# A selective-scan stage on one core: an output norm's shift and a copy moved to ScalarE, exponentials put ahead, and a residual taken apart on GpSimd

## The chip, the cores and the metric

The kernel runs on one core of a Trainium2 chip. The metric is the device time of one execution in microseconds (us); lower is better. Engines are named as in the profile: PE is TensorE, DVE is VectorE, ACT is ScalarE, POOL is GpSimd, SP is SyncE.

## The reference

Two layers on x of 16 x 256 x 128 (float32). Layer 0 is a retention recurrence and a mixture of experts, layer 1 a selective scan (Mamba) and a top-2 mixture of experts. The change touches the scan alone:

```python
# per sequence of 256 rows; h is the modulated layer norm of x
proj = h @ W_in.T                      # x_s (256), z (256), B (16), C (16), dt (8)
x_s  = silu(conv4(x_s) + conv_b)
dt   = softplus(dt @ W_dt.T + b_dt)
A    = -exp(A_log)
# for t in 256 steps, for each of 256 channels d and 16 states n:
#   S[d,n] = exp(dt[d] * A[d,n]) * S[d,n] + dt[d] * B[n] * x_s[d]
#   y[d]   = sum_n S[d,n] * C[n]
y    = (y + x_s * D) * silu(z)
out  = h + y @ W_out.T
out  = (out - mean) * rsqrt(var + 1e-5) * ln_g + ln_b
x    = x + ga * out
```

## The kernel before

`scan_phase` works through B = 16 sequences, one after the other. A sequence has 8 steps, j = 0 to 7 (SCAN_J), of two states each. In each engine's program `body(b, k, first, prepares)` is one sequence: it runs the 8 steps of sequence b, finishes sequence b-1 (its output product, norm and residual, `finish`) and prepares sequence b+1 (`prepare`). Every engine keeps its own fixed order, and semaphores join them. Sequence 0 finishes nothing, sequence 15 prepares nothing, and `last` finishes sequence 15.

One step j of sequence b: POOL writes dt*u*B, transposed, for two states into `dbuT` (`inputs`, four instructions, three steps ahead of use). PE turns it into a PSUM bank (`turn_inputs`). ACT writes exp(dt*A) into `dA` (`decays`, four instructions, three steps ahead, in a ring of four). DVE runs the recurrence over time (`recur`, one scan of 1024 elements, L1229) and multiplies by C (`times_C`, L1240). PE spreads C over the partitions (`C_rows`, L1614) and sums the states in PSUM (`sum_states`, L1644). In steps 0, 1 and 3 POOL takes half of the product with C (`shared_C`, L1498), and DVE's scan two steps later waits for it.

Preparing b+1: ACT normalises x (`xn`, L1279), PE transposes it, ACT modulates it to `hT` (L1285), PE projects it (L1550), ACT copies out the rows `low`, `BT` and `bc` (`prepare(1)`), and POOL splits `bc` into bfloat16 parts (`split`, L1419 to L1424, in its step 6). `C_rows(b+1, 0)` on PE waits for that split. PE projects the step sizes (L1560), ACT makes abs, positive part, exponential, square and logarithm of them (`prepare(2)`), POOL the cubic (`cubic`, L1435 and L1440), DVE the smaller of the two (`lesser`, L1200), POOL `dt` (L1446). PE runs the convolution (L1568), ACT loads the table of silu and makes `u` and `z` from it, loads its first table again (`prepare(4)`), makes `decays(7)` and then copies `dtuT` (L1319, `prepare(5)`), which PE has transposed (L1584) from POOL's `dtu` (L1460). POOL's `inputs(b+1, ..., 0)` starts in its step 5 and waits for `dtuT`. `hres` is a copy of `hT` for the residual product (`keep`, L1454).

Finishing b-1: DVE multiplies by z (`yz`, L1206), PE transposes it and multiplies by W_out (L1594 to L1604), DVE takes mean and variance of the output (`omv`, step 2), ACT the reciprocal deviation (`orstd`, L1329 and L1331), DVE the shift -mean*orstd (`oshift`, L1220), ACT the normalised output (`oh`, L1336), and POOL adds it to x with three instructions (`residual`, L1466, L1469, L1474) in its step 5, ahead of `inputs(b+1, ..., 0)`.

Of the kernel before, what the change touches and what calls it, by code (L numbers as in the profile page):

```python
# [20 lines left out]
P = 128  # L21
# [71 lines left out]
def pause(eng, passed):  # L93

    eng.sem_inc(passed, 1)
# [30 lines left out]
def setup_phase(nc, d, m, ps):  # L126

    with ExitStack() as ctx:
# [71 lines left out]
        def _(dve):  # L200
# [4 lines left out]
            tick(dve.memset(m.eps[:, 3:4], -SMALL_E))  # L205
            tick(dve.memset(m.eps[:, 4:5], SQ_B))
            tick(dve.memset(m.gates[:, 0, 2 * D:3 * D], 0.0))
            tick(dve.memset(m.ones128[:], 1.0 / D))
# [896 lines left out]
def scan_phase(nc, d, m, ps):  # L1105
# [8 lines left out]
    with ExitStack() as ctx:  # L1114
        sem = semaphores(nc, ctx, "s_")

        def sb(n, s, dt=F32):
# [4 lines left out]
        ostats, omv = sb("ostats", [P, NCH, 6]), sb("omv", [P, NCH, 2])  # L1122
        olnv, orstd, oshift = (sb(n, [P, NCH]) for n in ("olnv", "orstd", "oshift"))
        xn = sb("xn", [P, NCH, D])
# [25 lines left out]
                 "cub small least e_ready sq over st rs shift xn xT h hres xs_ps bc_ps z_ps low BT "  # L1150
                 "u_ready z_ready dt_ps pos abs ln soft dt_ready dtu_ready dtuT_ps dtuT hi r1 mid bc_parts oln gate "
                 "yz yzT_ps yzT out_ps ostats ost ors oshift o_read og done "
# [17 lines left out]
        def _(dve):  # L1170
# [31 lines left out]
            def finish(step, b, k):  # L1202
                if step == 0:
                    dve.wait_ge(S["y_part"], 8 * b + 8)
                    dve.wait_ge(S["z_ready"], b + 1)
                    dve.tensor_tensor(yz[:], bY[:, :].rearrange("p (c d) -> p c d", c=NCH), z[:, k], ALU.mult)\  # L1206
                        .then_inc(S["yz"], 1)
                if step == 2:
                    dve.wait_ge(S["out_ps"], b + 1)
                    pause(dve, S["v_passed"])  # L1210
                    for c in range(NCH):
                        dve.bn_stats(ostats[:, c, :], bZ[:, c * D:(c + 1) * D]).then_inc(S["ostats"], 1)
                    dve.wait_ge(S["ostats"], 2 * b + 2)
                    pause(dve, S["v_passed"])
                    for c in range(NCH):
                        dve.bn_aggr(omv[:, c, :], ostats[:, c, :]).then_inc(S["ost"], 1)
                if step == 3:
                    dve.wait_ge(S["ors"], b + 1)
                    dve.wait_ge(S["ost"], 2 * b + 2)
                    dve.scalar_tensor_tensor(oshift[:], omv[:, :, 0], -1.0, orstd[:], ALU.mult, ALU.mult)\  # L1220
                        .then_inc(S["oshift"], 1)

# [21 lines left out]
            def body(b, k, first, prepares):  # L1244
                for j in range(SCAN_J):
                    recur(b, j)
                    if not first and j != 3:
                        finish(j, b - 1, 1 - k)
                    if prepares and j == 4:
                        lesser(b + 1)  # L1250
                    times_C(b, j, first)
                    if not first and j == 3:
                        finish(j, b - 1, 1 - k)

# [9 lines left out]
        def _(act):  # L1264
# [8 lines left out]
            def prepare(step, b, k):  # L1273
# [43 lines left out]
                if step == 5:  # L1317
                    act.wait_ge(S["dtuT_ps"], b + 1)
                    act.activation(dtuT[:, k], bX[:, :].rearrange("p (c d) -> p c d", c=NCH), ACT.Copy)\  # L1319
                       .then_inc(S["dtuT"], 1)  # L1320

            def finish(step, b, k):
# [4 lines left out]
                if step == 2:  # L1327
                    act.wait_ge(S["ost"], 2 * b + 2)
                    act.activation(olnv[:], omv[:, :, 1], ACT.Ln, bias=m.eps[:, 0:1]).then_inc(S["oln"], 1)  # L1329
                    act.wait_ge(S["oln"], b + 1)  # L1330
                    act.activation(orstd[:], olnv[:], ACT.Exp, scale=-0.5).then_inc(S["ors"], 1)  # L1331
                if step == 3:
                    act.wait_ge(S["oshift"], b + 1)
                    act.wait_ge(S["og"], 2 * b + 2)
# [16 lines left out]
            def body(b, k, first, prepares):  # L1351
                for j in range(SCAN_J):
                    if prepares and j in (4, 5):
                        prepare(j, b + 1, 1 - k)
# [4 lines left out]
                    if prepares and j == 0:  # L1359
                        prepare(0, b + 1, 1 - k)  # L1360
                        prepare(0.5, b + 1, 1 - k)
                    if prepares and j == 1:
                        prepare(1, b + 1, 1 - k)
                        prepare(2, b + 1, 1 - k)
                    if not first:
# [7 lines left out]
            act.wait_ge(S["shift"], 1)  # L1373
            for j in (0, 0.5, 1, 2, 3, 4, 5):
                prepare(j, 0, 0)
                if j == 2:
                    rstds(1, NCH, TILES)
# [33 lines left out]
        def _(pool):  # L1411
# [35 lines left out]

            def keep(b, k):

                pool.wait_ge(S["h"], b + 1)  # L1450
                if not (isinstance(b, int) and b <= 1):
                    pool.wait_ge(S["out_ps"], b - 1)
                pause(pool, S["p_passed"])
                pool.tensor_copy(hres[:, k, :], hT[:, k, BACK:]).then_inc(S["hres"], 1)  # L1454

            def times_u(b, k):
# [4 lines left out]

            def residual(b):

                pool.wait_ge(S["o_read"], 2 * b + 2)
                pool.wait_ge(S["done"], b + 1)
                pool.tensor_tensor(og[:], oh[:], gate[:, 0, bass.ds(b, 1), :].broadcast_to([P, NCH, D]), ALU.mult)\  # L1466
                    .then_inc(S["og"], 1)
                pool.wait_ge(S["og"], 2 * b + 3)
                pool.tensor_tensor(og[:], og[:], gate[:, 1, bass.ds(b, 1), :].broadcast_to([P, NCH, D]), ALU.add)\  # L1469
                    .then_inc(S["og"], 1)  # L1470
                pool.wait_ge(S["og"], 2 * b + 4)
                pause(pool, S["p_passed"])
                xs = m.x_res[:, bass.ds(b * NCH, NCH), :]
                pool.tensor_tensor(xs, xs, og[:], ALU.add).then_inc(S["done"], 1)  # L1474

            def inputs(b, k, j, free):

# [5 lines left out]
                pause(pool, S["p_passed"])  # L1483
                for c in range(NCH):
                    for n in range(2):
                        ins = pool.tensor_scalar(dbuT[:, j % RING, c, n, :], dtuT[:, k, c, :],  # L1486
                                                 BT[:, k, c, 2 * j + n:2 * j + n + 1], 1.0, ALU.mult, ALU.mult)
                ins.then_inc(S["dbuT"], 1)
# [13 lines left out]
            def body(b, k, first, prepares):  # L1502
                for j in range(SCAN_J):
# [4 lines left out]
                    if not first and j == 5:  # L1508
                        residual(b - 1)
                    if j + AHEAD < SCAN_J:  # L1510
                        inputs(b, k, j + AHEAD, not (first and j + AHEAD < RING))
                    elif prepares:
                        inputs(b + 1, 1 - k, j + AHEAD - SCAN_J, True)
                    if prepares and j == 3:
# [3 lines left out]
                    if prepares and j == 6:  # L1518
                        split(b + 1, 1 - k)
                    if prepares and j == 7:  # L1520
                        keep(b + 1, 1 - k)

# [5 lines left out]
            split(0, 0)  # L1528
            keep(0, 0)
            cubic(0)  # L1530
            steps(0, 0)
            times_u(0, 0)
            for j in range(AHEAD):
                inputs(0, 0, j, False)
            sequences(pool, body, lambda b, k: residual(b))

# [999 lines left out]
```

## Time and profile before

| | before |
|---|---|
| device time, median of 3 runs | 1308.1 us (1304.93 to 1313.24) |
| profiled execution | 1306.6 us, of it a span of 1304.8 us from first to last instruction |
| busy share of the span | PE 79%, PEld 63%, DVE 63%, ACT 52%, POOL 47% |
| DVE's scans (L1229) | 128 in 291.6 us, from 401.4 us to 865.5 us |
| POOL's `dbuT` (L1486) | 512 in 242.3 us |
| mean granted clock of PE | 0.891 |

The span holds several stages in turn; the scan stage runs from about 380 to 880 us. Within it a sequence is a period that repeats, so most of the reading is of one period, from 606 to 636 us, and of the two ends of the stage. Busy shares of the whole span say little about it.

### The profile page before, as it was taken

Reading aid. Unit: us, or ns where it says so; the run is one execution under the profiler, and the core shown is the slowest. Engines: PE = TensorE matmul, PEld = TensorE weight load, DVE = VectorE, ACT = ScalarE, POOL = GpSimd, SP = SyncE. Lnnn points to the kernel's source line nnn. Section 1 sums busy time; section 2 is a strip of 40 time slices with the busy share of each in tenths; the row PEclk is TensorE's granted clock in tenths of the full one; section 3 lists DMA queues with packets and bytes.
Section 4 is the critical chain, followed back from the end, with each engine's and each line's share of the span. In section 5 each row is a group of like instructions: output and inputs, shape, how many; then the busy total and the mean of one; then the engine's idle time right before and its main releaser. Section 6 shows DMA issues by size and latency. Waiting matters only on the chain. (4 is left out here: it accounts for less than half of the span.)

```text
span 1304.8 us, 24618 instructions
## 1 busy us (share of the span) xinstructions
PE 1030.7 (79%) x7128; PEld 820.0 (63%) x7129; DVE 828.4 (63%) x1598; ACT 676.9 (52%) x1513; POOL 615.4 (47%) x922
## 2 busy tenths in 40 slices
PE   3999829999977888888898888851743999999950
PEld 2676623667867777888888778841732666666630
DVE  3787647222356999999999999961766333333327
ACT  2566313343127888888888888712642333333310
POOL 0000004000108899999999999930110455555630
PEclk9998759899978999999999999975555999999985
DMA  6000000766120000000000000005110111111135
GB/s 204 2 2 0 1 7 32 162 160 162 33 71 20 14 13 12 12 17 19 12 12 12 12 12 12 13 0 202 32 33 7 33 38 38 38 38 37 38 83 166
DMA packets 51613, 59.08 MB, mean 45 GB/s; under 512 B 5417, under 2 KB 45298, under 8 KB 50306
## 3 DMA queue, kind: packets, MB, share of 16 engines
q1 hardware_dynamic: 41570, 41.18, 11.9%
q0 software_dynamic: 4608, 9.45, 2.6%
q10 hardware_dynamic: 5392, 7.92, 1.8%
q8 instruction: 22, 0.36, 0.1%
q14 instruction: 21, 0.17, 0.0%
HBM read 49.32 MB, written 9.21 MB: 45 GB/s over the span
## 5 line engine op out<-in xcount | busy, mean ns | idle before, releaser
L1229 DVE TENSOR_TENSOR_SCAN s_hs<-s_dA,bank 128x1024 f32<-128x1024 f32 x128 | 291.6, 2278 | 9.8 <-PE bank L1626 9.1
L1486 POOL TENSOR_SCALAR s_dbuT<-s_dtuT,s_BT 128x256 f32<-128x256 f32 x512 | 242.3, 503 | 11.3 <-POOL s_bc L1424 5.4
L1347 ACT ACTIVATE s_dA<-s_dt,aneg 128x255 f32<-128x255 f32 x512 | 211.8, 495 | 0.3
L2255 PE MATMUL bank<-w,x_xT 128*128 x288 | 128.1, 568 | 18.0 <-ACT x_xT L2297 15.6
L1626 PE MATMUL bank<-const,s_dbuT 128*128 128x128 f32 x1024 | 136.0, 277 | 3.1 <-POOL s_dbuT L1486 3.1
L1240 DVE TENSOR_TENSOR s_hc<-s_hs,bank 128x1024 f32<-128x1024 f32 (+1 forms) x128 | 130.3, 1018 | 4.8 <-PE bank L1614 1.1
L1644 PE MATMUL bank<-const,s_hc 128*128 128x128 f32 x832 | 113.6, 275 | 21.1 <-DVE s_hc L1240 21.1
L2214 POOL DMA_INDIRECT x_xg<-hf_rows,x_src x72 | 69.7, 969 | 127.7 <-issue 63.9
L2293 ACT ACTIVATE x_a<-bank 128x448 f32<-128x448 f32 x72 | 39.2, 545 | 159.3 <-PE bank L2255 156.9
L1626 PEld LDWEIGHTS bank<-const,s_dbuT 128*128 128x128 f32 x1024 | 117.0, 143 | 6.3 <-POOL s_dbuT L1486 3.6
L1644 PEld LDWEIGHTS bank<-const,s_hc 128*128 128x128 f32 x832 | 95.0, 142 | 24.9 <-DVE s_hc L1240 24.9
L2221 POOL DMA_INDIRECT y_rows<-x_y,x_dst x72 | 71.1, 987 | 29.3 <-issue 22.4
L2255 PEld LDWEIGHTS bank<-w,x_xT 128*128 128x128 f32 x288 | 50.0, 193 | 55.1 <-issue 54.5
L2277 PE MATMUL bank<-w2d,x_hT 112*128 x576 | 77.6, 277 | 2.2 <-DVE x_y L2325 2.0
L2313 DVE COPY x_src<-from_row 128x1 uint32 (+1 forms) x72 | 11.1, 154 | 98.8 <-PE bank L2264 95.4
L2277 PEld LDWEIGHTS bank<-w2d,x_hT 112*128 112x128 f32 x576 | 69.9, 191 | 4.8 <-issue 4.2
L1031 DVE COPY yT<-bank 128x512 f32 x16 | 11.1, 692 | 91.7 <-PE bank L1011 91.7
L1023 ACT ACTIVATE g<-bank 128x512 f32<-128x512 f32 x64 | 38.2, 597 | 56.7 <-PE bank L1002 56.7
L1614 PE MATMUL bank<-s_bc,spread 128*128 128x256 bf16 x208 | 44.6, 277 | 27.1 <-DVE s_hc L1240 26.7
L1568 PE MATMUL bank<-s_hT,wc 128*128 128x256 f32 x256 | 62.4, 388 | 1.3 <-ACT s_pos L1300 1.3
L1498 POOL TENSOR_TENSOR s_hc<-s_hs,s_Crow 128x512 f32<-128x512 f32 x48 | 61.8, 1286 | 0.1
L1002 PE MATMUL bank<-xin,w 128*128 x128 | 59.4, 619 | 2.8 <-POOLq L973 2.8
(300 smaller groups left out, 2103.8 us busy)
## 6 DMA issues: line engine op xcount, KB each, us to landing
xn<-prob_d SPq DMA_DIRECT2D x16, 512.0 KB, 7.8
s_Crow<-C_rows SPq DMA_DIRECT2D x48, 128.0 KB, 2.9
w<-in_w SPq DMA_DIRECT2D x16, 256.0 KB, 3.1
o_yr<-y_rows SPq DMA_DIRECT2D x8, 512.0 KB, 3.9
w<-in_w ACTq DMA_DIRECT2D x1, 3584.0 KB, 13.1
x_res<-in_x SPq DMA_DIRECT2D x4, 512.0 KB, 9.4
gate<-gates_d SPq DMA_DIRECT2D x2, 1024.0 KB, 5.8
spread<-place_d SPq DMA_DIRECT2D x8, 256.0 KB, 6.4
```

The source lines that it names most:

```text
L1229: dve.tensor_tensor_scan(flat(hs[:, j % 2]), flat(dA[:, j % RING]), bDbu[j % 2], 0.0, ALU.mult, ALU.add).then_inc(S["scanned"], 1)
L1240: dve.tensor_tensor(hc[:, j % 2, :, 0:own], hs[:, j % 2, :, 0:own], bC[:, 0:own * L].rearrange("p (n t) -> p n t", n=own).unsqueeze(1).bro ...
L1347: ins = act.activation(dA[:, j % RING, h, n, 1:], dt[:, k, h, 1:], ACT.Exp, scale=m.aneg[:, h, 2 * j + n:2 * j + n + 1])
L1486: ins = pool.tensor_scalar(dbuT[:, j % RING, c, n, :], dtuT[:, k, c, :], BT[:, k, c, 2 * j + n:2 * j + n + 1], 1.0, ALU.mult, ALU.mult)
L1498: pool.tensor_tensor(hc[:, j % 2, :, 1], hs[:, j % 2, :, 1], Crow[:, k, i, :].unsqueeze(1).broadcast_to([P, NH, L]), ALU.mult)\
L1568: mm = pe.matmul(bX[:, h * L:(h + 1) * L], m.wc[:, tap, h * P:(h + 1) * P], hT[:, k, tap:tap + L], start=(tap == 0), stop=(tap == KCONV - 1))
L1626: mm = pe.transpose(out[:, h, n, c * P:(c + 1) * P], dbuT[:, j % RING, c, n, h * P:(h + 1) * P], ident)
L1644: mm = pe.matmul(part(c, h), hc[:, j % 2, h, n, c * P:(c + 1) * P], ident, is_transpose=True, start=(j == 0 and n == 0 and c == 0 and h == 0),
L2214: pool.indirect_dma_start(xg[k][:], None, m.hf_rows[:, :], bass.IndirectOffsetOnAxis(ap=src[k][:, 0:1], axis=0)).then_inc(S["rows"][k], 16)
L2221: pool.indirect_dma_start(m.y_rows[:, :], bass.IndirectOffsetOnAxis(ap=dst[k][:, 0:1], axis=0), y[k][:], None).then_inc(S["sent"][k], 16)
L2255: mm = pe.matmul(ps[2 * k + i][:, 0:I1], xT[:, k, :], m.w13[:, bass.ds(e * 2 + i, 1), :].rearrange("p e i -> p (e i)"), start=True, stop=True)
L2277: mm = pe.matmul(ps[5][:, 0:D], hT[:, k, i, :], m.w2d[:, bass.ds(e * NIC + i, 1), :].rearrange("p e d -> p (e d)"), start=(i == 0), stop=( ...
```

## The change

Four parts, all in `scan_phase`. (1) ACT computes `oshift` itself, with three small instructions behind `orstd` (a negated `orstd`, then one product for each half), and DVE's L1220 goes; with it goes the exception that put DVE's `finish(3)` behind `times_C`. (2) The copy `hres` goes from POOL (step 7) to ACT (`prepare(6)`, at the head of its step 6). (3) ACT's `prepare(2)` moves from step 1 to step 2, behind `decays(5)`. (4) POOL's `residual` becomes three functions: the first product (`residual_gated`) stays in front of `inputs(b+1, ..., 0)`, the other two instructions go between that block's four: ts, shifted, ts, added, ts, ts. A constant is also set once (`m.eps[:, 5:6]`) that nothing reads.

```diff
@@ DVE finish
-                if step == 3:
-                    dve.wait_ge(S["ors"], b + 1)
-                    dve.wait_ge(S["ost"], 2 * b + 2)
-                    dve.scalar_tensor_tensor(oshift[:], omv[:, :, 0], -1.0, orstd[:], ALU.mult, ALU.mult)\
-                        .then_inc(S["oshift"], 1)
@@ ACT prepare
+                if step == 6:
+                    act.wait_ge(S["h"], b + 1)
+                    if not (isinstance(b, int) and b <= 1):
+                        act.wait_ge(S["out_ps"], b - 1)
+                    act.activation(hres[:, k, :], hT[:, k, BACK:], ACT.Copy).then_inc(S["hres"], 1)
@@ ACT finish, step 2
                     act.activation(orstd[:], olnv[:], ACT.Exp, scale=-0.5).then_inc(S["ors"], 1)
+                    act.wait_ge(S["ors"], b + 1)
+                    act.activation(onegative[:], orstd[:], ACT.Copy, scale=-1.0).then_inc(S["onegative"], 1)
+                    act.wait_ge(S["onegative"], b + 1)
+                    for c in range(NCH):
+                        act.activation(oshift[:, c:c + 1], omv[:, c, 0:1], ACT.Copy, scale=onegative[:, c:c + 1])\
+                           .then_inc(S["oshift"], 1)
                 if step == 3:
-                    act.wait_ge(S["oshift"], b + 1)
+                    act.wait_ge(S["oshift"], 2 * b + 2)
@@ ACT body
-                    if prepares and j in (4, 5):
+                    if prepares and j in (4, 5, 6):
                         prepare(j, b + 1, 1 - k)
...
-                    if prepares and j == 1:
-                        prepare(1, b + 1, 1 - k)
-                        prepare(2, b + 1, 1 - k)
+                    if prepares and j in (1, 2):
+                        prepare(j, b + 1, 1 - k)
@@ POOL inputs
-            def inputs(b, k, j, free):
+            def inputs(b, k, j, free, rest=None):
...
-                for c in range(NCH):
-                    for n in range(2):
-                        ins = pool.tensor_scalar(dbuT[:, j % RING, c, n, :], dtuT[:, k, c, :],
-                                                 BT[:, k, c, 2 * j + n:2 * j + n + 1], 1.0, ALU.mult, ALU.mult)
+                for i in range(2 * NCH):
+                    c, n = divmod(i, 2)
+                    ins = pool.tensor_scalar(dbuT[:, j % RING, c, n, :], dtuT[:, k, c, :],
+                                             BT[:, k, c, 2 * j + n:2 * j + n + 1], 1.0, ALU.mult, ALU.mult)
+                    if rest is not None and i == 0:
+                        residual_shifted(rest)
+                    if rest is not None and i == 1:
+                        residual_added(rest)
@@ POOL body
                     if not first and j == 5:
-                        residual(b - 1)
+                        residual_gated(b - 1)
+                    if not first and j == 5 and not prepares:
+                        residual_shifted(b - 1)
+                        residual_added(b - 1)
...
-                        inputs(b + 1, 1 - k, j + AHEAD - SCAN_J, True)
+                        inputs(b + 1, 1 - k, j + AHEAD - SCAN_J, True, b - 1 if j == 5 and not first else None)
...
-                    if prepares and j == 7:
-                        keep(b + 1, 1 - k)
```

## Rows read from the trace of the kernel before

**Rows 1.** One period: us; busy PE, PEld, DVE, ACT, POOL; granted clock, DMA, GB/s.

```profile
520.00:549.00 29.00, 25.71 (x203) 23.29 (x202) 28.17 (x24) 24.65 (x56) 27.32 (x47) 1.00 0.07 14
```

**Rows 2.** Timeline of DVE, one period: start, us, engine, line, operation, [idle before].

```profile
606.07 2.28 DVE L1229 TENSOR_TENSOR_SCAN s_hs<-s_dA,bank 128x1024 f32<-128x1024 f32 x1
...
620.07 0.90 DVE L1220 SCALAR_TENSOR_TENSOR s_oshift<-s_omv,s_orstd 128x2 f32<-128x2 f32 x1 [0.49 <-ACT s_orstd L1331]
620.90 2.27 DVE L1229 TENSOR_TENSOR_SCAN s_hs<-s_dA,bank 128x1024 f32<-128x1024 f32 x1
...
635.17 2.28 DVE L1229 TENSOR_TENSOR_SCAN s_hs<-s_dA,bank 128x1024 f32<-128x1024 f32 x1
```

**Rows 3.** Timeline of POOL in the same period.

```profile
608.73 0.41 POOL L1454 COPY s_hres<-s_hT 128x256 f32<-128x256 f32 x1
...
625.97 1.28 POOL L1460 TENSOR_TENSOR s_dtu<-s_dt,s_u 128x512 f32<-128x512 f32 x1 [0.16 <-POOL s_dt L1446]
627.20 0.73 POOL L1466 TENSOR_TENSOR s_og<-s_oh,s_gate 128x256 f32<-128x256 f32 x1
628.12 0.73 POOL L1469 TENSOR_TENSOR s_og<-s_og,s_gate 128x256 f32<-128x256 f32 x1 [0.18 <-POOL s_og L1466]
629.12 0.73 POOL L1474 TENSOR_TENSOR x_res<-x_res,s_og 128x256 f32 x1 [0.27 <-POOL s_og L1469]
629.83 3.67 POOL L1486 TENSOR_SCALAR s_dbuT<-s_dtuT,s_BT 128x256 f32<-128x256 f32 x8
...
635.00 0.67 POOL L1424 TENSOR_TENSOR s_bc<-s_r,s_bc 32x256 bf16<-32x256 f32 x1
```

**Rows 4.** Timelines of DVE and POOL around other executions of L1220.

```profile
445.15 1.27 POOL L1440 TENSOR_TENSOR s_small<-s_cub,s_e 128x512 f32<-128x512 f32 x1
...
445.21 1.23 DVE L1220 SCALAR_TENSOR_TENSOR s_oshift<-s_omv,s_orstd 128x2 f32<-128x2 f32 x1 [0.32 <-ACT s_orstd L1331]
...
852.14 0.79 DVE L1220 SCALAR_TENSOR_TENSOR s_oshift<-s_omv,s_orstd 128x2 f32<-128x2 f32 x1
...
875.93 0.16 DVE L1220 SCALAR_TENSOR_TENSOR s_oshift<-s_omv,s_orstd 128x2 f32<-128x2 f32 x1 [0.60 <-ACT s_orstd L1331]
```

**Rows 5.** Timeline of ACT in the same period.

```profile
624.54 0.84 ACT L1311 ACTIVATE s_u<-bank,bcol 128x256 f32<-128x256 f32 x2 [0.92 <-PE bank L1568]
...
628.92 0.57 ACT L1319 ACTIVATE s_dtuT<-bank 128x512 f32<-128x512 f32 x1
629.40 6.47 ACT L1347 ACTIVATE s_dA<-s_dt,aneg 128x255 f32<-128x255 f32 x16
```

**Rows 6.** Timelines of POOL, PE, ACT: end of sequence 0, sequence 1.

```profile
426.18 3.66 POOL L1486 TENSOR_SCALAR s_dbuT<-s_dtuT,s_BT 128x256 f32<-128x256 f32 x8 [2.93 <-ACT s_dtuT L1319]
...
431.43 0.67 POOL L1424 TENSOR_TENSOR s_bc<-s_r,s_bc 32x256 bf16<-32x256 f32 x1
...
425.37 0.58 ACT L1319 ACTIVATE s_dtuT<-bank 128x512 f32<-128x512 f32 x1
...
454.07 0.57 ACT L1319 ACTIVATE s_dtuT<-bank 128x512 f32<-128x512 f32 x1
...
432.23 0.28 PE L1614 MATMUL bank<-s_bc,spread 128*128 128x256 bf16 x1 [0.36 <-POOL s_bc L1424]
...
447.75 1.89 PE L1568 MATMUL bank<-s_hT,wc 128*128 128x256 f32 x8
```

**Rows 7.** Timelines of DVE, POOL, PE: both ends of the stage.

```profile
437.68 2.29 DVE L1229 TENSOR_TENSOR_SCAN s_hs<-s_dA,bank 128x1024 f32<-128x1024 f32 x1 [0.66 <-POOL s_hc L1498]
...
845.03 2.28 DVE L1229 TENSOR_TENSOR_SCAN s_hs<-s_dA,bank 128x1024 f32<-128x1024 f32 x1
...
833.40 3.66 POOL L1486 TENSOR_SCALAR s_dbuT<-s_dtuT,s_BT 128x256 f32<-128x256 f32 x8
...
404.43 0.44 PE L1545 MATMUL bank<-const,s_xn 128*128 128x128 f32 x2 [1.66 <-ACT s_xn L1279]
```

**Rows 8.** Groups of instructions, 433 to 836 us: busy, mean ns, idle before.

```profile
L1331 ACT ACTIVATE s_orstd<-s_olnv 128x2 f32<-128x2 f32 x14 | 2.9, 204 | 0.4
```

More of the change, by code:

```diff
@@ L206, in _ @@
             tick(dve.memset(m.eps[:, 4:5], SQ_B))
+            tick(dve.memset(m.eps[:, 5:6], SQ_C))
             tick(dve.memset(m.gates[:, 0, 2 * D:3 * D], 0.0))
@@ L1122, in scan_phase @@
         ostats, omv = sb("ostats", [P, NCH, 6]), sb("omv", [P, NCH, 2])
-        olnv, orstd, oshift = (sb(n, [P, NCH]) for n in ("olnv", "orstd", "oshift"))
+        olnv, orstd, onegative, oshift = (sb(n, [P, NCH]) for n in ("olnv", "orstd", "onegative", "oshift"))
         xn = sb("xn", [P, NCH, D])
@@ L1150, in scan_phase @@
                  "cub small least e_ready sq over st rs shift xn xT h hres xs_ps bc_ps z_ps low BT "
-                 "u_ready z_ready dt_ps pos abs ln soft dt_ready dtu_ready dtuT_ps dtuT hi r1 mid bc_parts oln gate "
+                 "u_ready z_ready dt_ps pos abs ln soft dt_ready dtu_ready dtuT_ps dtuT hi r1 mid bc_parts oln onegative gate "
                  "yz yzT_ps yzT out_ps ostats ost ors oshift o_read og done "
@@ L1246, in body @@
                     recur(b, j)
-                    if not first and j != 3:
+                    if not first:
                         finish(j, b - 1, 1 - k)
@@ L1251, in body @@
                     times_C(b, j, first)
-                    if not first and j == 3:
-                        finish(j, b - 1, 1 - k)
             def last(b, k):
@@ L1373, in _ @@
             act.wait_ge(S["shift"], 1)
-            for j in (0, 0.5, 1, 2, 3, 4, 5):
+            for j in (0, 0.5, 1, 2, 3, 4, 5, 6):
                 prepare(j, 0, 0)
@@ L1446, in steps @@
                 pool.tensor_tensor(dt[:, k], least[:], pos[:], ALU.add).then_inc(S["dt_ready"], 1)
[L1448 to L1454, printed above, removed]
             def times_u(b, k):
@@ L1460, in times_u, with residual_gated @@
                 pool.tensor_tensor(dtu[:], dt[:, k], u[:, k], ALU.mult).then_inc(S["dtu_ready"], 1)
-            def residual(b):
+            def residual_gated(b):
                 pool.wait_ge(S["o_read"], 2 * b + 2)
@@ L1467, in residual, with residual_shifted @@
                     .then_inc(S["og"], 1)
+            def residual_shifted(b):
                 pool.wait_ge(S["og"], 2 * b + 3)
@@ L1470, in residual, with residual_added @@
                     .then_inc(S["og"], 1)
+            def residual_added(b):
                 pool.wait_ge(S["og"], 2 * b + 4)
-                pause(pool, S["p_passed"])
                 xs = m.x_res[:, bass.ds(b * NCH, NCH), :]
                 pool.tensor_tensor(xs, xs, og[:], ALU.add).then_inc(S["done"], 1)
-            def inputs(b, k, j, free):
+            def inputs(b, k, j, free, rest=None):
                 if j == 0:
@@ L1528, in _ @@
             split(0, 0)
-            keep(0, 0)
             cubic(0)
@@ L1534, in _, with last @@
                 inputs(0, 0, j, False)
-            sequences(pool, body, lambda b, k: residual(b))
+            def last(b, k):
+                residual_gated(b)
+                residual_shifted(b)
+                residual_added(b)
+            sequences(pool, body, last)
         @block.tensor
```

## Prediction

> **What bounds the kernel now.** I read the busy time by engine in one period first, then the timelines of DVE and POOL, then what ends the short idle times. In 29.00 us DVE is busy 28.17 and POOL 27.32, PE 25.71, ACT 24.65 [rows 1]: two engines are full, so busy shares alone don't say which one sets the pace. The period is the distance of two first scans, 635.17 - 606.07 = 29.10 us [rows 2].
>
> POOL's timeline [rows 3] has no idle time that another engine ends. Its gaps (0.16, 0.18, 0.27) are waits for its own instruction before. POOL's period is thus a sum of its own work. DVE has one soft place: before L1220 it waits 0.49 us for ACT, and L1220 then takes 0.90 us on 2 columns [rows 2]. The same instruction took 0.16 us when POOL was idle, and 1.23 us when it began at 445.21; it ended at 446.44, just as POOL's L1440 did (445.15 + 1.27 = 446.42) [rows 4]. So L1220 stands still until POOL's running instruction is over, and this is where DVE, which is a little faster, is held back to POOL's pace. **POOL bounds the period, and DVE is tied to it at L1220.**
>
> The Trainium skill says the same of this ("SBUF — State Buffer", section "SBUF: two separate sides": a VectorE operation with two SBUF inputs and a GpSimd operation take an exclusive lock, and the loser blocks for the whole instruction). Read alone, it speaks for a large gain of part (1), which is the rival "DVE's pace" below; L1220's rows agree with the rule, but the sum below doesn't need it.
>
> The third thing to see is how near POOL is to a wait. `dtuT` ends at 628.92 + 0.57 = 629.49 on ACT [rows 5], and POOL starts `inputs(b+1, 0)`, which waits for it, at 629.83 [rows 3]. POOL's residual, 627.20 to 629.85, fills the time until `dtuT` is there. It costs nothing at that place.
>
> **Part 1, oshift on ACT.** DVE loses the wait and L1220. Idle began at 620.07 - 0.49 = 619.58 and the next scan started at 620.90: 1.32 us per sequence, so DVE alone could run a sequence in 27.8 us. ACT gains three instructions on 1 or 2 columns; the nearest row is 0.204 us for L1331 on the same columns [rows 8], with the waits between them some 0.55 us. Below it they could be shorter by overlap, above it 0.8. It lies in slack: ACT waits 0.92 us for the convolution before `u` [rows 5], and part 3 adds to that wait. Only in `last`, where nothing covers it, it shows: 0.55 against DVE's 0.16 and two crossings, +0.35 us once. DVE isn't the bound, so the 1.3 us turn into waiting of DVE elsewhere: next late is either the scan of step 2, which waits for POOL's first `shared_C` (it waited 0.66 us in sequence 1 [rows 7]), or `lesser`, with two SBUF inputs too, behind POOL's `shared_C(3)`.
>
> **Part 2, hres on ACT.** POOL loses 0.41 us per sequence [rows 3]. ACT gains some 0.40 (an exponential of 255 columns is 6.47/16 [rows 5]). On ACT it stands between `dtuT` and `xn`. At the beginning of the stage PE waits 1.66 us for `xn` [rows 7], so there the 0.40 passes through, once.
>
> **Part 3, exponentials first.** `decays(5)` (1.6 us) moves into ACT's wait for PE's step-size projection. That projection isn't earlier, so abs, positive part and the rest start when they did. ACT then reaches `u` earlier and waits longer for the convolution. Price nought, and if the cover were gone (projection ready before the exponentials end) up to 1.6 us on ACT, none of it on the path below.
>
> **Part 4, residual apart.** POOL's gaps of 0.18 and 0.27 vanish [rows 3], as each dependent instruction has one of `dbuT` (0.46) before it. With part 2 POOL's own work falls to 29.10 - 0.41 - 0.45 = 28.24 us. But the two instructions no longer stand ahead of the wait for `dtuT`; they stand behind it, between the instructions whose results it gates. They cost 629.83 - 629.12 = 0.71 us each [rows 3]: the step-0 block grows from 1.83 to 1.83 + 1.42 = 3.25 us, and nothing runs on POOL between the end of `residual_gated` and `dtuT`. Queued behind this wait on POOL are `inputs(b+1, 1)`, the split and everything else.
>
> **The loop that closes.** Let X be the end of `inputs(b, 0)`. All terms but the last two are seen together in sequence 1, in which POOL was late:
> - X to the end of the split: 635.67 - (629.83 + 1.83) = 4.01 us [rows 3]; in sequence 1, 432.10 - 428.01 = 4.09 [rows 6].
> - PE's `C_rows(b, 0)` waits for the split and starts 0.13 us later, at 432.23; from there PE runs to the end of the convolution at 447.75 + 1.89 = 449.64: 17.41 us [rows 6]. In that stretch PE has no time to catch up.
> - ACT: silu, its second table load, `decays(7)` and `dtuT`, until 454.07 + 0.57 = 454.64: 5.00 us [rows 6].
> - POOL starts 0.23 us after `dtuT` (426.18 - 425.95) [rows 6].
> - the block itself, now 3.25 us.
>
> 4.01 + 0.13 + 17.41 + 5.00 + 0.23 + 3.25 = **30.03 us**. Without the interleaving it is 28.61, below POOL's own 29.10, which is why it doesn't show before. Now it is the longest loop: +0.93 us per sequence, and POOL waits some 1.7 us for `dtuT` in each. In the steady period before, `C_rows(b, 0)` was set by DVE, not by the split; DVE has 1.3 us less to do and comes early, so the split decides.
>
> X moves so from sequence 1 to sequence 15: 14 periods, 14 x 0.93 = +13.0 us. Beginning +0.40, end +0.35. In sequence 15 DVE gains: its third scan, at X + 9.80 before (845.03 - 835.23), can go at X + 9.67 - 0.41 (sequence 1's 437.68 - 428.01, less the copy) [rows 6, 7], -0.54, and L1220's 0.79 is nearly all gone [rows 4], -0.7. Sum: 13.0 + 0.75 - 1.2 = **+12.5 us**. Against the profiled execution, 1306.6 (span 1304.8 and 1.8 around it), it gives 1319.1; that execution lies 1.5 us under the median of the runs, so against 1308.1 it is 1320.6. Predicted: 1320.
>
> **Rivals.**
> *POOL's own work stays the bound.* If `dtuT` came as early as POOL wants it, the period would be 28.24 us: 14 x -0.86 - 1.2 + 0.75 = -12.5, 1295.6. It needs `dtuT` 1.7 us earlier. For it: POOL has no foreign wait in the steady period. Against: ACT's last 5 us hang on PE's convolution, and nothing on PE is shortened. *DVE's pace* (1.3 us off each of 15 sequences, 1288) is the skill's rule taken alone; POOL's 28.24 exclude it. Together 0.08.
> *The two cancel.* Parts 2 and 4 give back 0.86 us of POOL's time; if the loop is 0.9 us shorter than my sum, because with early DVE and ACT the stretch from `C_rows` to the convolution has less waiting in it than the 0.30 to 0.49 us I see, or because DVE and not the split still starts it, the period stays 29.1: 1307 to 1309. 0.17.
> *POOL's switches cost.* Changing between the two kinds of instruction, with a wait at each change, could cost 0.1 to 0.2 us each (POOL starts `dtuT`'s dependent 0.23 us late) instead of nothing, four changes per sequence: +0.4 to 0.8 us more, 1326 to 1331. It decides if the six instructions of the block span over 3.6 us. Against it: the residual's last instruction runs into `dbuT` without a gap. 0.15.
> The forecast itself has 0.6, between 1316 and 1324: an error of 0.1 us in a term is 1.4 us.
>
> **Chances.** A measurement of this kernel tells about 1% from no change, 13 us. The forecast lies just at that bound, so its 0.6 is shared, 0.31 within and 0.29 beyond. Faster 0.08; within 1%: 0.17 + 0.31 = 0.48; slower 0.15 + 0.29 = 0.44. The range of 8 in 10 leaves out the first rival and half of the third: 1304 to 1326. The forecast's own range is 1316 to 1324.
>
> **What would show it.** In the profile after: the first instruction of L1486's step-0 block idle before it for 1.5 to 1.8 us, ended by ACT's `dtuT`, in 14 sequences; `C_rows(b, 0)` on PE waiting for POOL's split each time; the period at 30.0 us; DVE with some 2 us of idle time, at the third scan and at the smaller-of-two; POOL's busy time per period about 28. ACT's wait before L1299 gone and that before `u` 2 us. Wrong if POOL has no wait for `dtuT` (then the first rival), or if the scans start as before at 29.1 us.

## The result, and the profile after

The changed kernel took 1328.05 us (median of 5 runs, 1317.46 to 1332.45) against 1311.06 us before (now 5 runs, 1304.93 to 1313.24): a ratio of 1.011, 95% interval 1.0076 to 1.0145. It is slower by 1.1%; 1.0% had been forecast. Taken as it stands, the median of 1328.05 lies above the forecast's own range, 1316 to 1324, and above 1326; the two medians differ by 1.3%, a little more than the ratio says. Its profiled execution took 1317.46 us, with a span of 1315.7. One of the ten executions of e7 below took 1835.74 us at a granted clock of 0.553, and its ratio is that of the other nine.

I compare the scan stage by the distance of successive starts of `dtuT` on ACT, which is the period of one sequence, in one profiled execution of each kernel. Before, the mean of the last 13 periods is 29.11 us; after, 30.09. First POOL's timeline of one period after (start, us, engine, line, operation, idle before), which answers to [rows 3]:

```profile
633.50 0.48 POOL L1487 TENSOR_SCALAR s_dbuT<-s_dtuT,s_BT 128x256 f32<-128x256 f32 x1 [2.19 <-ACT s_dtuT L1313]
633.94 0.73 POOL L1468 TENSOR_TENSOR s_og<-s_og,s_gate 128x256 f32<-128x256 f32 x1
...
635.09 0.72 POOL L1475 TENSOR_TENSOR x_res<-x_res,s_og 128x256 f32 x1
635.79 2.75 POOL L1487 TENSOR_SCALAR s_dbuT<-s_dtuT,s_BT 128x256 f32<-128x256 f32 x6
...
640.03 0.67 POOL L1428 TENSOR_TENSOR s_bc<-s_r,s_bc 32x256 bf16<-32x256 f32 x1
```

POOL, which waited for nobody in [rows 3], now stands still for 2.19 us until `dtuT` is there. The gaps inside the residual are gone, but its last two instructions run after the wait. The last two of the block's four instructions are the first two of the row at 635.79; they took 0.94 us, so the block ends at 636.73. PE's timeline and ACT's, of the same round:

```profile
634.59 0.39 PE L1624 MATMUL bank<-s_bc,spread 128*128 128x256 bf16 x2 [0.72 <-DVE s_hc L1236]
636.85 1.09 PE L1636 MATMUL bank<-const,s_dbuT 128*128 128x128 f32 x8 [1.87 <-DVE s_hs L1225]
637.78 1.91 PE L1654 MATMUL bank<-const,s_hc 128*128 128x128 f32 x16
...
640.76 0.28 PE L1624 MATMUL bank<-s_bc,spread 128*128 128x256 bf16 x1 [1.07 <-POOL s_bc L1428]
...
656.25 1.89 PE L1578 MATMUL bank<-s_hT,wc 128*128 128x256 f32 x8
```

```profile
658.18 0.84 ACT L1305 ACTIVATE s_u<-bank,bcol 128x256 f32<-128x256 f32 x2 [1.76 <-PE bank L1578]
...
662.57 0.58 ACT L1313 ACTIVATE s_dtuT<-bank 128x512 f32<-128x512 f32 x1
```

The fourth PE row is `C_rows` of step 0: it waits for POOL's split, which [rows 6] showed once and the steady period before not at all. The 1.87 us of the second row are put down to DVE's scan, which ended at 636.73 too; but that product needs DVE's scan of step 6, long done by then, and POOL's block, which ended at 636.73. Where a wait names an instruction that isn't needed, look at who else ended then. The loop, term by term: block's end to split's end 640.70 - 636.73 = 3.97; to `C_rows` 0.06; to the end of the convolution 658.14 - 640.76 = 17.38; to the end of `dtuT` 663.15 - 658.14 = 5.01; to POOL's next start (663.43) 0.28; the block 636.73 - 633.50 = 3.23. Sum 29.93, forecast 30.03.

DVE in the same kernel, its third scan and its smaller-of-two, which answer to [rows 2, 4]:

```profile
645.99 2.29 DVE L1225 TENSOR_TENSOR_SCAN s_hs<-s_dA,bank 128x1024 f32<-128x1024 f32 x1 [0.92 <-POOL s_hc L1503]
...
655.32 1.16 DVE L1201 TENSOR_TENSOR s_least<-s_small,s_soft 128x512 f32<-128x512 f32 x1
```

Its small instruction and that one's wait are gone; 0.92 us come back as a wait for POOL's shared product, and the smaller-of-two takes 1.16 us instead of 0.67, with POOL at work on a product until 654.66 + 1.27 = 655.93. DVE gained nothing.

Last, the granted clock, which I hadn't foreseen. Busy time by stretch in the changed kernel (columns as in [rows 1]), two of the later sequences:

```profile
572.70:602.90 30.20, 27.26 (x203) 25.15 (x201) 28.07 (x23) 25.55 (x60) 26.84 (x45) 0.94 0.05 13
633.20:663.10 29.90, 25.89 (x203) 23.48 (x201) 28.12 (x23) 25.56 (x61) 26.84 (x45) 1.00 0.06 13
```

Seven of the 13 periods have a mean clock of 0.94. Five of these last 30.25 to 30.26 us and two 29.93 and 30.02; the six at 1.00 last 29.94 to 30.04. In the five, PE's 16 matmuls behind the second wait took up to 3.48 us instead of 1.91, and `C_rows` of step 0 started 0.34 to 0.49 us behind the split instead of 0.06 or 0.13, without waiting for it. There the loop closes over PE, which is itself late. The first period took 32.11 us here at 0.73, and 28.72 before at 0.88. From the first `dtuT` to the end of `oh` the stage takes 17.7 us more (480.3 to 497.9): 3.4 in the first period, 14.3 behind it. In this execution the stage's first `xn` came 5.5 us earlier than before (at 374.09 instead of 379.58), though ahead of it nothing is changed but a constant that nothing reads.

### The profile page after: what moved, and what is told of

It is laid out like the page before. It is cut to its first block and busy times, and to the rows that moved or that the text cites. A ratio compares the mean times of both kernels' runs of the same rounds, so it can differ in the third digit from the quotient of the medians.

```text
span 1315.7 us, 24617 instructions
## 1 busy us (share of the span) xinstructions
PE 1037.8 (79%) x7128; PEld 831.4 (63%) x7129; DVE 825.8 (63%) x1583; ACT 690.6 (52%) x1577; POOL 606.8 (46%) x906
## 5 line engine op out<-in xcount | busy, mean ns | idle before, releaser
L1636 PE MATMUL bank<-const,s_dbuT 128*128 128x128 f32 x1024 | 142.1, 285 | 29.0 <-DVE s_hs L1225 25.9
L1636 PEld LDWEIGHTS bank<-const,s_dbuT 128*128 128x128 f32 x1024 | 121.8, 147 | 34.8 <-DVE s_hs L1225 29.8
L1654 PE MATMUL bank<-const,s_hc 128*128 128x128 f32 x832 | 120.1, 290 | 2.9 <-DVE s_hc L1236 2.9
L1654 PEld LDWEIGHTS bank<-const,s_hc 128*128 128x128 f32 x832 | 105.1, 152 | 3.4 <-DVE s_hc L1236 3.4
L1012 PEld LDWEIGHTS bank<-w,g 128*128 128x128 f32 x512 | 58.4, 192 | 3.8 <-issue 3.8
```

The source lines that it names most:

```text
L1636: mm = pe.transpose(out[:, h, n, c * P:(c + 1) * P], dbuT[:, j % RING, c, n, h * P:(h + 1) * P], ident)
L1654: mm = pe.matmul(part(c, h), hc[:, j % 2, h, n, c * P:(c + 1) * P], ident, is_transpose=True, start=(j == 0 and n == 0 and c == 0 and h == 0),
```

## The experiments

Periods are the mean of the last 13 distances of `dtuT`, "first" is the first distance; ratios are to the kernel before, timed on the same chip, with their 95% interval.

| run | edit | period, us | first | ratio |
|---|---|---|---|---|
| before | | 29.11 | 28.72 | 1 |
| changed | parts 1 to 4 | 30.09 | 32.11 | 1.011 (1.0076 to 1.0145) |
| e1 | parts 1 to 3 | 28.85 | 28.99 | 0.9987 (0.9966 to 1.0008) |
| e2 | part 4 | 30.10 | 31.89 | 1.0108 (1.0065 to 1.015) |
| e3 | part 1 | 28.91 | 28.72 | 1.0004 (0.9986 to 1.0022) |
| e4 | part 2 | 28.89 | 32.13 | 0.9996 (0.9975 to 1.0018) |
| e11 | part 3 | 28.90 | 31.99 | 0.9973 (0.9955 to 0.9991) |
| e7 | part 4, two blocks later | 29.66 | 28.99 | 1.0047 (1.0023 to 1.007) |
| e8 | changed, PE kept busy | 29.99 | 32.04 | 1.0072 (1.0045 to 1.01) |
| e10 | changed, dtuT earlier | 29.78 | 31.46 | 1.0068 (1.0048 to 1.0089) |
| e5 | e1, gated ahead of dtu | 28.85 | 32.13 | 0.9968 (0.9936 to 1.0) |
| e6 | e5, split ahead of block 0 | 29.58 | 32.13 | 1.0045 (1.0023 to 1.0067) |
| e9 | e5, dtuT earlier | 30.66 | 31.45 | 1.0165 (1.0136 to 1.0195) |
| e12 | e5, hres in POOL's wait | 28.63 | 31.97 | 0.9918 (0.989 to 0.9946) |

**e1, part 4 undone.**

```diff
                     if not first and j == 5:
                         residual_gated(b - 1)
-                    if not first and j == 5 and not prepares:
                         residual_shifted(b - 1)
                         residual_added(b - 1)
...
-                        inputs(b + 1, ..., True, b - 1 if j == 5 and not first else None)
+                        inputs(b + 1, ..., True)
```

> The changed kernel with part 4 alone undone: all three residual instructions stand again ahead of the wait for dtuT. Theory (part 4 closes the loop over the split, PE, ACT and dtuT): the loop is 30.03 - 1.42 = 28.61 us, POOL's own work 29.10 - 0.41 = 28.69, so the period is 28.7 us, 0.4 below the kernel before; 14 periods give 1301 to 1304 us, and POOL's wait for dtuT is gone or under 0.2 us. Rival (the instructions that ScalarE gained, or the new order of its exponentials, lengthen the period): it stays at 30 us and the time at 1318 to 1328, with POOL still waiting 1.5 us or more. Rival (DVE's pace, now that its small instruction is gone): 27.8 us, about 1290.

The period falls by 1.24 us, to 28.85. Part 4 is the cause of the loss. (The change also leaves out a `pause` in front of the residual's last instruction, which the diff above doesn't show. e1 leaves it out too; POOL then stands idle there for 0.19 us instead of 0.27.) The rest, expected at 28.7, is 0.15 longer. e1's own rows say why. From the start of `dtuT` at 598.77 ACT works without a gap until the end of `xn` at 606.79, 8.02 us, and PE's transposes of `xn` start 0.06 us later:

```profile
606.85 0.44 PE L1554 MATMUL bank<-const,s_xn 128*128 128x128 f32 x2
```

From there the convolution's end is 16.34 us away, at 623.19, and the next `dtuT` starts 4.42 us behind that: 28.84 together. This is a round over ACT and PE alone. Without the copy it is 0.30 us shorter (`dtuT` to the end of `xn` took 7.72 us before).

**e2, part 4 alone on the kernel before.**

```diff
-                        residual(b - 1)
+                        residual_gated(b - 1)
...
-                        inputs(b + 1, ..., True)
+                        inputs(b + 1, ..., True, b - 1 if j == 5 and not first else None)
```

> The kernel before with part 4 alone: the residual's last two instructions between those of the step-0 block. Theory: the same loop, 30.0 us per period with the copy still on POOL and the small instruction still on DVE, +13 us, 1320 to 1324; POOL waits for dtuT in 14 sequences, by some 1.3 us (0.4 less than in the changed kernel, since the copy is still there). Rival (only parts 1 to 3 together make DVE early enough for the split to decide): period 29.1, 1308 to 1311.

The whole loss, with the same two kinds of period. POOL's step-0 block waits here too, 1.53 us with the clock at full speed before it:

```profile
635.79 0.48 POOL L1491 TENSOR_SCALAR s_dbuT<-s_dtuT,s_BT 128x256 f32<-128x256 f32 x1 [1.53 <-ACT s_dtuT L1319]
```

The rival that parts 1 to 3 must first make DVE early is out.

**e3, part 1 alone** (DVE's `finish(3)` out, ACT's three instructions in, as in the change's diff).

> The kernel before with part 1 alone: oshift on ScalarE, VectorE's small instruction gone. Theory (POOL's own work is the bound, VectorE is only tied to it): period 29.1 us, time as before within 3 us (1305 to 1312); VectorE's 1.3 us come back as waits, at the third scan for POOL's shared product and as a longer smaller-of-two (L1200 over 0.67 us, blocked by POOL). Rival (VectorE's pace): 27.8 us, 1288 to 1292.

Ratio 1.0004, and DVE's time comes back as foreseen, 0.63 us as a wait for POOL at the third scan and the rest here:

```profile
621.79 1.16 DVE L1200 TENSOR_TENSOR s_least<-s_small,s_soft 128x512 f32<-128x512 f32 x1
```

The period is 0.2 us under 29.11 all the same: POOL's last `dbuT` block, in which DVE's smaller-of-two falls, took 2.16 us here and 2.27 before, and its other instructions a few ns less each (the 39 shared products 1278 ns, before 1287). The difference of 0.11 lies in one instruction, the one beside the smaller-of-two: 0.91 us before, 0.80 here. In both it ended 0.34 to 0.35 us behind DVE's; DVE's now runs right behind POOL's product, and before it ran one instruction of POOL later.

**e4, part 2 alone** (`keep` out of POOL, `prepare(6)` into ACT, as in the change's diff).

> The kernel before with part 2 alone: the copy hres on ScalarE. Theory (POOL bound): the period falls by the copy's 0.41 us to 28.69, 14 x 0.41 = 5.7 us faster, 1302 to 1305, and VectorE's small instruction is less long (it stood still for POOL, 0.90 us before, about 0.5 now). Rival (VectorE and PE bound as much as POOL): period 29.1, 1307 to 1310, and POOL has idle time instead.

Half of what was expected: 0.22 us per period instead of 0.41, too little for the timed ratio. POOL now starts its step-0 block 0.29 us behind `dtuT` (631.94 + 0.58 on ACT), the distance at which it starts when it has waited for it:

```profile
632.81 1.38 POOL L1483 TENSOR_SCALAR s_dbuT<-s_dtuT,s_BT 128x256 f32<-128x256 f32 x3 [0.16 <-issue]
```

So there was another round at 28.85 to 28.9 us close under POOL's 29.1, the one of e1, and I had put the next at 28.6.

**e11, part 3 alone.**

```diff
-                    if prepares and j == 1:
-                        prepare(1, b + 1, 1 - k)
-                        prepare(2, b + 1, 1 - k)
+                    if prepares and j in (1, 2):
+                        prepare(j, b + 1, 1 - k)
```

> The kernel before with part 3 alone: the exponentials of step 5 ahead of prepare(2). Theory (ScalarE isn't in the way of anything that is late): ScalarE's wait before L1299 falls from 1.7 us to about 0.1 and that before the silu grows by as much; VectorE's small instruction no longer waits for orstd but still for POOL; period 28.9 to 29.1, ratio 0.998 to 1.000. Rival (it lengthens the way to the step sizes): period over 29.2.

A gain of 0.2 us per period, as in e3 and on the same ground: DVE's small instruction finds `orstd` ready by 1.3 us, takes 231 ns in the mean, and DVE waits for POOL at the third scan instead. POOL's instruction beside the smaller-of-two takes 0.80 us here too. ACT's wait ahead of `prepare(2)` fell from 1.70 to 0.53 to 0.60 us, not to 0.1.

**e7, the same interleaving two blocks later.**

```diff
-                        inputs(..., b - 1 if j == 5 and not first else None)
+                        inputs(..., b - 1 if j == 7 and not first else None)
```

> The changed kernel with the same two residual instructions between the same kind of instructions, but in the block of step 2 (POOL's step 7), behind the split, instead of step 0. Theory (not the interleaving costs, but its place between dtuT and the split): the 1.42 us leave the loop over the split, C_rows, convolution and dtuT; what is left is that loop at 28.6 to 28.9 us, or POOL's own 28.2 plus the idle time behind residual_gated until dtuT, about 28.9. Period 28.9, ratio to the kernel before 0.995 to 1.000. Rival (interleaving itself, by switches of instruction or register waits, costs the time): period 30.1 as in the changed kernel, ratio 1.011.

29.66: between theory and rival. POOL and then DVE:

```profile
603.78 3.67 POOL L1487 TENSOR_SCALAR s_dbuT<-s_dtuT,s_BT 128x256 f32<-128x256 f32 x8 [1.50 <-ACT s_dtuT L1313]
...
610.43 0.73 POOL L1468 TENSOR_TENSOR s_og<-s_og,s_gate 128x256 f32<-128x256 f32 x1
...
615.01 1.27 POOL L1503 TENSOR_TENSOR s_hc<-s_hs,s_Crow 128x512 f32<-128x512 f32 x1
```

```profile
616.31 2.29 DVE L1225 TENSOR_TENSOR_SCAN s_hs<-s_dA,bank 128x1024 f32<-128x1024 f32 x1 [1.34 <-POOL s_hc L1503]
```

PE shows no wait for the split, and the period is 0.3 us under that of the changed kernel's fastest sequences, so the place matters. But the two instructions still stand ahead of POOL's shared product; DVE's third scan waits for that, PE's `C_rows` of step 3 waited 0.50 us for DVE, and behind it come the same convolution and `dtuT`. By the terms: block 1.83, blocks 1 to 3, split and shared product 615.01 + 1.27 - 605.61 = 10.67, scan to product 4.30, `C_rows` of step 3 to convolution 628.14 - 620.67 = 7.47, 5.00 to the end of `dtuT`, 0.3 to POOL: 29.57 with the crossings left out. The loop isn't one chain but a bundle; work between `dtuT` and POOL's first shared product lies on one of them wherever it stands.

**e8, PE kept busy while it waits.**

```diff
-                for n in range(1 if j in SHARED else 2):
+                for n in [0, 1] * (5 if j == 7 else 1) if j not in SHARED else [0]:
                     mm = pe.matmul(bC[:, n * L:(n + 1) * L], m.spread[:, 2 * j + n, :], bc[:, k, :], ...)
```

> The changed kernel with the product that spreads C in step 7 written five times instead of once (the same values to the same place, 8 matmuls more, some 0.9 us of PE in the time in which it waits 1.9 us for dbuT). Theory (in the changed kernel some periods are 30.26 us at a mean granted clock of 0.94 and others 29.94 to 30.04 at 1.00, and PE's new idle time in front of these is what the clock falls after): the clock stays 1.00 from sequence 1 on, all periods are 29.9 to 30.05, and the time is 2 to 6 us under the changed kernel's; ratio to the kernel before 1.007 to 1.009. Rival (the clock falls for another reason): periods of 30.26 as often as before, ratio 1.011.

All 13 periods lie at 29.94 to 30.05, none at 30.25. One of them by busy time:

```profile
580.00:610.00 30.00, 26.87 (x212) 24.37 (x211) 28.22 (x23) 25.65 (x61) 26.85 (x45) 1.00 0.05 13
```

With 0.9 us of PE's wait filled the clock stays at 1.00 in all 13. The time can't confirm it: 1.0072 against 1.011, on another chip, with intervals that overlap.

**e10, dtuT ahead of the exponentials of step 7, in the changed kernel.**

```diff
-                    if prepares and j in (4, 5, 6):
+                    if prepares and j in (4, 6):
                         prepare(j, b + 1, 1 - k)
+                    if prepares and j == 4:
+                        prepare(5, b + 1, 1 - k)
```

> The changed kernel (interleaving kept) with ScalarE's copy of dtuT ahead of the exponentials of step 7 instead of behind them. In the changed kernel's trace PE's transposes of dtu end at 631.91 and ScalarE is at the exponentials until 632.63, so dtuT can be 0.67 us earlier. Theory (ScalarE's stretch from the convolution to dtuT is a link of the loop that sets the period): every period falls by 0.6 to 0.7 us, from 29.94-30.26 to 29.3-29.6, ratio to the kernel before 1.003 to 1.006. Rival (the loop runs elsewhere, over VectorE or POOL alone): periods as in the changed kernel, ratio 1.011.

29.78, all periods alike: 0.16 to 0.48 less instead of 0.6 to 0.7. ACT's stretch is a link, but ACT now waits 0.94 us for PE's transposes with all its exponentials behind it, and the next round is at 29.78. The clock fell to a mean of 0.94 in five of the 13 periods and none got longer by it: PE's lateness is hidden where another round bounds.

**e9** has the same edit on e5.

> The kernel of e5 (residual whole again, its first instruction ahead of dtu) with ScalarE's copy of dtuT ahead of the exponentials of step 7. Theory: the loop of 28.85 us loses 0.58 (PE's transposes end 0.6 us before ScalarE is free in e5), POOL's wait of 0.66 us falls to about 0.1, period 28.27, just above POOL's own work of 28.2: 14 x (29.09 - 28.27) + 0.7 = 12 us less than the kernel before, ratio 0.990. Rival (VectorE then waits for the exponentials of step 7, which come 0.2 us before their use now, or for POOL's shared product): 28.8 us, ratio 0.997.

Slower than everything else, and the clearest row of the study, ACT and PE:

```profile
615.12 0.60 ACT L1313 ACTIVATE s_dtuT<-bank 128x512 f32<-128x512 f32 x1 [0.94 <-PE bank L1596]
...
623.90 0.86 ACT L1273 ACTIVATE s_xn<-x_res,s_shift,s_rstd 128x128 f32 x2
```

```profile
624.81 0.44 PE L1557 MATMUL bank<-const,s_xn 128*128 128x128 f32 x2 [1.52 <-ACT s_xn L1273]
```

PE waits for `xn`. It is the round of e1: `dtuT`, the exponentials and `hres`, `xn`, PE's transposes to the convolution, silu, second table load, `dtuT`. The four exponentials of step 7, ahead of `dtuT` in e1, now stand behind it, so 20 of them lie between `dtuT` and `xn` instead of 16. With 0.94 us of waiting in it it takes 29.78 here as in e10, so 28.84 without: that is the 28.85 to 28.89 of e1, e4 and e5, in all three of which PE's transposes start 0.05 to 0.06 us behind `xn`. It holds the copy of part 2. The other seven periods of e9, 31.40 to 31.43, come with a mean clock of 0.95.

**e5, residual_gated ahead of dtu.**

```diff
+                    if not first and j == 5:
+                        residual_gated(b - 1)
                     if prepares and j == 5:
                         times_u(b + 1, 1 - k)
                     if not first and j == 5:
-                        residual_gated(b - 1)
                         residual_shifted(b - 1)
```

> The kernel of e1 with residual_gated ahead of dtu, which hides two waits of POOL for itself (0.17 and 0.18 us). Theory (e1 is bound by the loop over dtuT: POOL waited 0.3 us for it in each sequence): POOL has 0.35 us less to do and waits 0.65 instead of 0.34; period unchanged at 28.85. Rival (POOL's own work bounds e1 too): 28.5 us, 5 us faster than e1.

The period is e1's to 0.01 us, POOL's wait for `dtuT` 0.66: POOL's own work doesn't bound e1.

**e6, the split in POOL's wait.**

```diff
@@ POOL split
                 if not (isinstance(b, int) and b == 0):
-                    pool.wait_ge(S["dbuT"], 8 * b + 2)
+                    pool.wait_ge(S["dtu_ready"], b + 1)
@@ POOL body
                     if prepares and j == 5:
                         times_u(b + 1, 1 - k)
+                        split(b + 1, 1 - k)
...
-                    if prepares and j == 6:
-                        split(b + 1, 1 - k)
```

> The kernel of e5 with the split for the next sequence moved from POOL's step 6 into the time in which dtuT is on its way (behind dtu, ahead of the other two residual instructions). Theory (the split is a link of the loop and POOL's wait is the place to do it in): PE's C_rows of step 0 never waits for the split, the loop loses its 2.2 us, POOL has no wait for dtuT, and the period is POOL's own work, 28.85 - 0.34 - 0.35 = 28.2 us, VectorE's 27.8 just below it. 14 x (29.09 - 28.2) = 12.5 us less than the kernel before, with 0.7 of the last sequence: ratio 0.990. Rival (VectorE, tied to POOL by the shared product and the smaller-of-two, adds its waits to 27.8 and bounds): 28.8, ratio 0.998.

It failed. The split is 2.3 us long and the wait was 0.66, so the step-0 block starts 1.45 to 1.48 us behind `dtuT` instead of 0.29, and PE waits for it as in the changed kernel:

```profile
611.09 1.15 PE L1635 MATMUL bank<-const,s_dbuT 128*128 128x128 f32 x8 [1.66 <-POOL s_dbuT L1487]
612.03 3.55 PE L1653 MATMUL bank<-const,s_hc 128*128 128x128 f32 x16
```

Five periods are 28.84 to 28.86, at a mean clock of 1.00, and eight 29.95 to 30.05, at 0.94. The second row shows the difference: 16 matmuls behind the wait took 3.55 us, where the five have 1.91, as the changed kernel at 637.78. The wait itself, 1.64 to 1.66 us, is the same in both kinds. So the later block costs nothing here where the clock holds, and 1.2 us where it falls.

**e12, hres back on POOL, in its wait.**

```diff
@@ ACT body
-                    if prepares and j in (4, 5, 6):
+                    if prepares and j in (4, 5):
                         prepare(j, b + 1, 1 - k)
@@ POOL body
                         residual_added(b - 1)
+                    if prepares and j == 5:
+                        keep(b + 1, 1 - k)
```

> The kernel of e5 with the copy hres back on POOL, at the end of the residual, in POOL's wait of 0.66 us for dtuT. Theory (e1, e4 and e5 all have periods of 28.85 to 28.88 us because ScalarE's own round, dtuT, 16 exponentials, the copy, xn, then PE's transposes to the convolution, silu and dtuT again, is that long; the copy's 0.31 us are in it): the round falls to 28.55, the loop over the split stands at 28.61, POOL's own work at 28.2 + 0.4 = 28.6. Period 28.6, 14 x (29.09 - 28.6) + 0.7 = 7.6 us less than the kernel before, ratio 0.994. Rival (another engine's round, or the split, bounds e5): 28.85, ratio 0.997.

28.57 to 28.68, and 0.8% faster than the kernel before, where 0.6% was expected; the interval, 0.5 to 1.1%, holds both. PE's transposes now start 0.25 us behind `xn`: the round over ACT and PE no longer bounds. It is the fastest of all; of the others only e11 (0.9973) has an interval that lies wholly below 1.

## Why the prediction was right

- **What bounds before** holds. POOL sets the period; without L1220 (e3) DVE was no faster, only waiting elsewhere. The rival of DVE's pace, 1288 us, is out.
- **Part 4's loop** is right in mechanism and size: 29.93 measured term by term against 30.03, and e1 and e2 show that part 4 does it alone. The interleaved pair costs 1.40 us in its block (3.23 against 1.83), forecast 1.42. The rival "switches cost", which wanted over 3.6 us, is out. Of its signs some were off: POOL's wait is 1.86 to 2.19 us instead of 1.5 to 1.8, its busy time 26.84 instead of about 28, and `C_rows` waits for the split in the six periods at full clock, not each time.
- **The period**: +0.98 us against +0.93, of it 0.1 by a lower clock in five periods. The clock had no term in the sum. From the end of the step-0 block of sequence 1 to that of sequence 15 the kernel takes 14.4 us more (407.2 to 421.6), where 13.0 had been forecast.
- **Part 2** was mis-sized. "On ACT it stands between dtuT and xn" was seen, and priced only at the stage's beginning; it is also part of ACT's and PE's own round. I took the loop without the interleaving for 28.61, the next best after POOL's 29.10; the next one was ACT's, 28.85. So parts 1 to 3 together gave 0.26 us per period (29.11 to 28.85), not 0.41 and more. Under part 4 this doesn't show.
- **Part 3** was put at nought. Alone it gives 0.2 us per period (e11), as part 1 does (e3). About half of it, 0.11 us, is the one POOL instruction beside DVE's smaller-of-two, which meets it at another moment once DVE doesn't wait at L1220. Why others of POOL's instructions get shorter by some ns isn't shown.
- **The ends**: the last sequence gained 0.65 us, not 1.24 (its third scan starts at X + 9.86, not earlier than before, after DVE waited 0.81 and 1.13 us for PE), `last` cost 0.55, not 0.35. The copy's price at the beginning, put at 0.40, is 0.27 in the first period (28.72 to 28.99 in e1) and again 0.28 in the second (28.70 to 28.98). The rest of the first sequence's +3.4 us goes with the clock of that stretch, 0.73 against 0.88. Sequence 0 has no residual, so part 4 does nothing in it; and kernels without part 4 show both 28.7 to 29.0 (before, e1, e3) and 31.5 to 32.1 (e4, e5, e6, e9, e11, e12).

The forecast was 12.5 us, the profiled execution moved by 10.9, the medians by 17, the ratio by 1.1% with an interval of 0.8 to 1.5%. That 10.9 lies so near 12.5 is partly luck: the stage grew by 17.7 us, 3.4 of it in the first period, and its beginning happened to come 5.5 us earlier. The mechanism and the size per period are what the runs bear out. The granted clock of the timed executions falls as their time grows, 0.884 at 1317 us and 0.877 at 1332.

## What to carry to other kernels

An engine that never waits isn't proof that its order is free: ask, for each instruction, whether it stands before or behind the next wait. Work ahead of a wait fills it; the same work behind it is on the path, and here two instructions moved by one position cost 1.0 us in 29. When the bound is taken down, compute every round that closes over the engines, not only the next; here three lay between 28.6 and 29.1 us (POOL's own work at 29.1, ACT's and PE's at 28.85, the split's at 28.61 by its terms), and only e12, which shortened the second and filled the wait that remained, gained more than 0.5%.

## What the runs showed of the hardware

- PE's granted clock fell from 1.00 to 0.50 for a stretch in seven of 13 periods of the changed kernel, where PE stands idle for 0.72 and 1.87 us with one pair of small matmuls between (mean 0.94 in the period, 16 matmuls in up to 3.48 us, 3.55 in e6, instead of 1.91). The other six have the same idle times and kept the clock; what decides between them isn't shown. It fell in none of the last 14 periods of the kernel before, whose idle times there were 1.3 us each with some 2 us of matmuls between, and in none of e8's 13, where PE is kept busy for 0.9 us of the wait. A wait on another engine can so cost twice: 0.3 us more in the changed kernel, 1.2 in e6, 1.6 in e9, and nothing in e10, where another round bounds.
- POOL starts an instruction 0.23 to 0.30 us after the ACT result that it waited for, PE 0.06 or 0.13 after POOL's. DVE's L1201, 0.67 us in the kernel before, took 1.16 in the changed one, where it began inside a product of POOL, and ended 0.55 us behind that product; POOL's next instruction took 0.80 us instead of 0.48 and ended 0.35 us behind DVE's. The Trainium skill ("SBUF — State Buffer", "SBUF: two separate sides") says that whichever starts first, a VectorE operation with two SBUF inputs or a GpSimd operation that reads SBUF, holds a lock for the whole instruction, and the other is blocked. By that rule both would be held up as here, and the trace agrees.
